# Two stacked graph networks on one core: layer 0 of the next block runs ahead of layer 1, and its rows reach VectorE through SBUF instead of TensorE's transposes

## The chip, the core and the metric

The kernel runs on one core of a Trainium2 chip. The metric is the device time in microseconds (us), the median of several runs. A core has TensorE (PE, the matrix engine), VectorE (DVE), ScalarE (ACT), GpSimd (POOL) and SyncE (SP, which here only issues DMA transfers). Each engine runs its own list of instructions in order, and the lists meet at semaphores only.

## The reference, cut to what matters

The input `x` has 128 graphs of 64 nodes with 384 features, all float32. A first network (two layers) is followed by a residual and a layer norm, then a second network (two layers) with a residual and a layer norm. The change is in the second network:

```python
def layer(h, params):                      # twice
    u = jnp.einsum('bid,bjd->bij', h, h) / temper
    a = jax.nn.softmax(u, axis=-1)
    delta = a * adjacency_matrix
    attn = delta / (jnp.sum(delta, axis=-1, keepdims=True) + 1e-10)
    hl, hs, hr = h @ wl.T + b_l, h @ ws.T + b_s, h @ wr.T + b_r
    ctx = (attn * upper) @ hl + diag(attn)[..., None] * hs + (attn * lower) @ hr
    o = (ctx - mean) / jnp.sqrt(var + LN_EPS) * g + beta
    return jax.nn.relu(o)
```

Both the scores and the values need `h` with the features on the partitions, that is, transposed. For layer 0 the rows come from DRAM (`x1`, the first network's result), for layer 1 from layer 0 of the same block.

## The kernel before

The 8192 rows are cut into 16 blocks of 512 rows (`TOK`), each four tiles of 128. Two blocks ("streams" 0 and 1) make a pass, so there are `PASSES` = 8. Each pass of the second network has four **units** (`UNITS`): layer 0 of stream 0, layer 0 of stream 1, layer 1 of stream 0, layer 1 of stream 1, numbered 0 to 3. The network has 32 units in all. Passes 1 to 6 are a hardware loop on most engines; the others are written out.

TensorE sets the pace. In a unit (`one_pass`, L1244) it folds the score parts (`fold_parts`, L1197), multiplies twelve value products, numbered 0 to 11 (`values`, L1215: nine matmuls each, three sides times four tiles), transposes the exponentials after value 3 if the unit is of layer 1 (`turn_exponentials`, L1208), computes the scores of the next unit (`scores`, L1192), and at last multiplies the four context tiles (`contexts`, L1232).

If the next unit is of layer 1, TensorE also transposes that block's rows between the values: `turn_block` (L1176), twelve transposes of 128x128, eight after value 8 and four after value 9. They read `z`, into which ScalarE's `normalise` (L1363) wrote the rows of layer 0. If the next unit is of layer 0, the rows were loaded from DRAM in quarters (`load_x`, L1123, four transfers) such that VectorE's 32x32 block transposes give the same result: `flip_block` (L1610, three instructions for one unit).

Either way ScalarE then takes the turned block out of PSUM (`turn_out`, L1282) and VectorE writes its low part (`turn_lo`, L1603). In layer 0 ScalarE makes one pass over each of the three parts; in layer 1 it makes two, because gain, shift and relu are applied there (`gain_f`, `shift_f`, a value for each feature).

The four banks `work` form a ring. A value product with a bias needs a bank that ScalarE has filled with the bias (`seed`, L1323), and that waits until VectorE has read the bank four products earlier (`biased_value`, L1627, or `contexts_out`, L1661). So seeds 0 and 1 of a unit wait for VectorE's `contexts_out` of the unit before. ScalarE's order at the start of a unit is `first_half` (L1371). In layer 1 it is seed 0, 1, 3, value 0, the four exponentials, value 1, seed 4. Those exponentials wait for the row maximum, which VectorE takes at the end of the unit before, after `contexts_out` and `variances`, if the next unit is of layer 1 (`begin`, L1847).

After a layer-1 unit its block is finished during the unit that follows: GpSimd applies gain and shift (`times_gain`, `plus_shift`), VectorE adds the residual and takes the last statistics (`add_residual`, L1746, `final_stats`, L1753, `final_var`, L1758), all of it ahead of `contexts_out`; GpSimd normalises one unit later (`final_normalise`, L1546), and SP stores. A unit with this extra work on VectorE is called heavy in what follows. In the kernel before the heavy units are 3 and 0 of the next pass: both are followed by a unit of layer 0.

SP's list (`one_pass`, L1139) loads the residual rows, the next pass's rows and adjacency, and stores the results. The order of work on every engine is written out by hand.

Of the kernel before, what the change touches and what calls it, by code (L numbers as in the profile page):

```python
# [7 lines left out]
ALU = mybir.AluOpType  # L8
# [14 lines left out]
QUADS = P // QUAD  # L23

# [99 lines left out]
def gated_layers(nc, ctx, sh, x, x_t, adj, adj_t, w_left, w_right, w_lin_t, b_lin, ln_a, ln_b, table, x1,  # L124
# [26 lines left out]
    with ExitStack() as overlaid:  # L151
# [98 lines left out]
        def sync_program(sp):  # L250
# [77 lines left out]
            def next_tables():  # L328
                for m in range(3):
                    sp.dma_start(sh.bias[:, m], next_b[m].partition_broadcast(P)).then_inc(next_small, 16)  # L330
                sp.dma_start(sh.gain_f[:], next_ln_w[0].rearrange("(k p) -> p k", p=P),
                             allow_slow_non_contiguous=True).then_inc(next_small, 16)
                sp.dma_start(sh.shift_f[:], next_ln_b[0].rearrange("(k p) -> p k", p=P),
                             allow_slow_non_contiguous=True).then_inc(next_small, 16)
# [661 lines left out]
def softmax_layers(nc, ctx, sh, gated, x1, adj_t, w_nbr_t, table, out):  # L996
# [17 lines left out]
    assert LAYERS == 2 and WN * UNITS % RING == 0 and UNITS * KO % 2 == 0  # L1014
# [8 lines left out]
    with ExitStack() as block_ctx:  # L1023
# [81 lines left out]
        def layer_of(unit):  # L1105
            return unit % UNITS // STREAMS

        def in_layer(i, unit):

            return (i + unit // UNITS) * STREAMS + unit % STREAMS + 1  # L1110
# [6 lines left out]
        def _(sp):  # L1117
            store_last = gated_sync(sp)

            def load_weight(n):  # L1120
                sp.dma_start(stage[n], w_nbr_t[n][1].rearrange("(k p) o -> p k o", p=P)).then_inc(stage_in[n], 16)

            def load_x(i, s):  # L1123
                for q in range(QUADS):
                    sp.dma_start(sh.x_blocks[s][quarter(q)], x_b[i, s, q]).then_inc(x_loaded[s], 16)

            def load_adj(i, s):
                for b in range(2):
                    h = slice(b * 64, b * 64 + 64)
                    sp.dma_start(a_tr[s][h, :, h], adj_t_v[i, s, b]).then_inc(adj_loaded[s], 16)  # L1130
# [3 lines left out]
            load_weight(1)  # L1134
            sp.wait_ge(split, 1)
# [3 lines left out]
            def one_pass(i, last, first=False):  # L1139
                for s in range(STREAMS):  # L1140
                    wait(sp, summed, i * (STREAMS * NT) + (s + 1 - STREAMS) * NT)
                    sp.dma_start(x_res[s][:], x_v[i, s]).then_inc(x_copied[s], 16)
                    if not last:
                        sp.wait_ge(turned, nth(i, s, KO, KO - 1))
                        load_x(i + 1, s)
                for s in range(STREAMS):
                    if not last:
                        sp.wait_ge(keep_ready[s], i + 1)
                        load_adj(i + 1, s)
# [822 lines left out]
```

## Time and profile before

| quantity | value |
|---|---|
| median of 3 runs | 1693.14 us (1692.88 to 1693.48) |
| profiled execution, its own time | 1695.46 us |
| span of that execution, first to last instruction | 1693.6 us |
| mean granted TensorE clock | 0.995 of full speed |
| TensorE busy | 1668.7 us, 99% |
| VectorE busy | 1267.6 us, 75% |
| ScalarE busy | 956.0 us, 56% |
| GpSimd busy | 623.2 us, 37% |

The busy time of an engine counts a stretch in which several of its instructions overlap once. Matmuls overlap, so the mean duration of one is longer than its share of the time. The second network begins at about 839 us of the span and takes the rest. The span and the profiled execution's own time differ by 1.9 us, which lie around the first and the last instruction.

### The profile page before, as it was taken

The page shows a single profiled execution, that of the slowest core. Times are in us where ns is not written, and L with a number is a line of the kernel's source. Part 1 is how long each engine was busy: PE and PEld are TensorE (multiplying, and loading weights), DVE is VectorE, ACT ScalarE, POOL GpSimd, SP SyncE. Part 2 cuts the span into 40 slices and gives each one's busy share as a digit, 9 for nine tenths or more (in the row PEclk, how much of TensorE's full clock was granted, in tenths as well). Part 3 has the DMA queues.
Part 4 walks back from the last instruction along what each step waited for, and adds up shares of the span by engine and source line. Part 5 has one row for each costly group of instructions (what it writes and reads, how often), then busy time and mean ns, then how long its engine had stood idle before and what let it go on. Part 6 is the DMA issues. An engine that isn't in the chain of part 4 may idle for free.

```text
span 1693.6 us, 29852 instructions
## 1 busy us (share of the span) xinstructions
PE 1668.7 (99%) x9684; PEld 1580.2 (93%) x9684; DVE 1267.6 (75%) x2778; ACT 956.0 (56%) x2009; POOL 623.2 (37%) x668
## 2 busy tenths in 40 slices
PE   9999999999999999999999999999999999999995
PEld 8989989889899899899999999999999999999995
DVE  5587685867859678695887968769687686877866
ACT  5645455364554645546566665565655656656654
POOL 5243252433424233243523514434153351523505
PEclk9999999999999999999999999999999999999998
DMA  5215021020300203003104140400304004040101
GB/s 160 77 30 158 6 71 53 25 93 6 109 14 25 93 6 118 6 25 94 49 15 97 41 96 0 118 0 22 96 22 96 0 25 92 22 96 0 49 30 38
DMA packets 108074, 92.02 MB, mean 54 GB/s; under 512 B 63360, under 2 KB 101248, under 8 KB 108032
## 3 DMA queue, kind: packets, MB, share of 16 engines
q1 hardware_dynamic: 108032, 91.51, 19.1%
q8 instruction: 20, 0.33, 0.1%
q14 instruction: 22, 0.18, 0.0%
HBM read 66.33 MB, written 25.17 MB: 54 GB/s over the span
## 4 chain that ended last, share of the span: by engine, by line
PE 93%; DVE 3%; ACT 1%; POOL 1%; DMA 1%; issue 1%; SPq 0%; ACTq 0%; DVEq 0%
PE b_work L1228 33%; PE b_work L377 23%; PE b_work L402 11%; PE b_score_ps L392 8%; PE b_work L1241 8%; PE b_work L413 4%; PE b_score_ps L119 3%; PE b_turn L360 1%; PE b_turn L1185 1%; PE b_score_ps L1204 1%; DMA b_z<-in_L_gnn_W_lin 1%; PE b_score_ps L1201 0%; POOL g_qv_lo L663 0%; PE b_turn L1212 0%; PE b_score_ps L1185 0%
## 5 line engine op out<-in xcount | busy, mean ns | idle before, releaser
L1228 PE MATMUL b_work<-b_w_hi,b_ht 128*128 128x384 f32 x2304 | 605.2, 337 | 0.5 <-ACT b_work L1327 0.3
L1228 PEld LDWEIGHTS b_work<-b_w_hi,b_ht 128*128 128x128 f32 x2304 | 417.5, 188 | 1.7 <-ACT b_work L1327 1.2
L1228 PE MATMUL b_work<-b_w_lo,b_ht 128*128 128x384 f32 x1152 | 385.3, 334 | 0.0
L377 PE MATMUL b_work<-b_ht,b_w_hi 128*128 128x512 f32 x1134 | 350.5, 390 | 0.7 <-DVE g_qv_lo L782 0.7
L663 POOL TENSOR_TENSOR g_qv_lo<-g_v_full,g_qv_hi 128x384 fp32r<-128x384 f32 x128 | 132.8, 1057 | 359.2 <-ACT g_qv_hi L533 359.2
L377 PEld LDWEIGHTS b_work<-b_ht,b_w_hi 128*128 128x128 f32 x1134 | 211.8, 188 | 41.8 <-issue 1.1
L377 PE MATMUL b_work<-b_ht,b_w_lo 128*128 128x512 f32 x567 | 221.6, 391 | 0.0
L1228 PEld LDWEIGHTS b_work<-b_w_lo,b_ht 128*128 128x128 f32 x1152 | 216.5, 188 | 0.0
L1633 DVE TENSOR_TENSOR s_v_lo<-b_work,s_v_hi 128x384 fp32r<-128x384 f32 x256 | 140.7, 555 | 90.3 <-ACT s_v_hi L1333 86.6
L402 PE MATMUL b_work<-b_w_hi,b_ht 128*128 128x384 f32 x768 | 206.1, 335 | 0.0
L1327 ACT ACTIVATE b_work<-b_bias 128x384 f32<-128x384 f32 x256 | 126.4, 494 | 140.0 <-DVE b_z L1671 104.5
L782 DVE TENSOR_TENSOR g_qv_lo<-b_work,g_qv_hi 128x512 fp32r<-128x512 f32 x192 | 128.4, 686 | 98.4 <-ACT g_qv_hi L521 96.5
L521 ACT ACTIVATE g_qv_hi<-b_work 128x512 fp32r<-128x512 f32 x192 | 111.0, 592 | 124.1 <-PE b_work L377 124.0
L1333 ACT ACTIVATE s_v_hi<-b_work 128x384 fp32r<-128x384 f32 x256 | 123.8, 490 | 87.4 <-PE b_work L1228 87.2
L392 PE MATMUL b_score_ps<-g_qv_hi,b_ht 128*128 128x256 f32 x768 | 146.1, 284 | 0.0
L402 PEld LDWEIGHTS b_work<-b_w_hi,b_ht 128*128 128x128 f32 x768 | 139.7, 188 | 1.3
L402 PE MATMUL b_work<-b_w_lo,b_ht 128*128 128x384 f32 x384 | 128.6, 335 | 0.0
L377 PEld LDWEIGHTS b_work<-b_ht,b_w_lo 128*128 128x128 f32 x567 | 106.4, 188 | 22.6
L392 PEld LDWEIGHTS b_score_ps<-g_qv_hi,b_ht 128*128 128x128 f32 x768 | 120.9, 188 | 0.4
L1495 POOL TENSOR_TENSOR s_rstd<-s_var,s_power 128x4 f32<-128x4 f32 x31 | 31.3, 1009 | 235.2 <-DVE s_var L1690 235.2
L525 ACT ACTIVATE g_prob<-g_score_l 128x512 f32<-128x512 f32 x32 | 20.3, 634 | 159.8 <-DVE g_score_l L794 159.8
L392 PE MATMUL b_score_ps<-g_qv_lo,b_ht 128*128 128x256 f32 x384 | 107.2, 279 | 0.0
(174 smaller groups left out, 3288.1 us busy)
## 6 DMA issues: line engine op xcount, KB each, us to landing
g_x_res<-in_x SPq DMA_DIRECT2D x16, 768.0 KB, 7.7
b_x_in<-x SPq DMA_DIRECT2D x64, 192.0 KB, 6.7
s_x_res<-x SPq DMA_DIRECT2D x16, 768.0 KB, 7.3
b_x_in<-in_x_t SPq DMA_DIRECT2D x15, 768.0 KB, 8.9
out<-b_z SPq DMA_DIRECT2D x15, 768.0 KB, 3.8
x<-b_z SPq DMA_DIRECT2D x14, 768.0 KB, 3.9
b_a_tr<-in_adj_t SPq DMA_DIRECT2D x64, 64.0 KB, 3.3
g_a_nat<-in_adj SPq DMA_DIRECT2D x32, 64.0 KB, 2.4
```

The costliest lines, as they stand in the source:

```text
L377: mm = pe.matmul(bank[:], w, h, start=(n == 0), stop=(n == len(pairs) - 1))
L392: mm = pe.matmul(score_ps[:, t, :, :], h, q, start=(n == 0), stop=(n == len(pairs) - 1))
L402: mm = pe.matmul(bank[:, 0:H], h, w, start=(n == 0), stop=(n == len(pairs) - 1))
L413: mm = pe.matmul(bank[:, 0:HC], p[:, t, :], v[:, t, :], start=(n == 0), stop=(n == 2))
L521: nc.scalar.activation(q_hi[:, m, :, d, :], work[use % RING][:], ACT.Copy).then_inc(q_hi_ready, 1)
L663: nc.gpsimd.tensor_tensor(v_lo[:, t, 0:H], v_full[:, t, :], v_hi[:, t, 0:H].bitcast(F32), ALU.subtract).then_inc(v_lo_ready, 1)
L782: op = nc.vector.tensor_tensor(q_lo[:, m, :, d, :], bank, q_hi[:, m, :, d, :].bitcast(F32), ALU.subtract)
L1228: mm = pe.matmul(bank[:, 0:H], h, w, start=(n == 0 and side == 2), stop=(n == len(pairs) - 1), skip_group_check=True)
L1241: mm = pe.matmul(bank[:, 0:HC], p, v, start=(n == 0), stop=(n == len(pairs) - 1))
L1327: nc.scalar.activation(work[(unit * WN + j) % RING][:, 0:H], bias[:, side, layer_of(unit), :], ACT.Copy)\
L1333: nc.scalar.activation(v_hi[:, t, side, 0:H], work[(unit * WN + j) % RING][:, 0:H], ACT.Copy)\
L1633: nc.vector.tensor_tensor(v_lo[:, t, side, 0:H], bank[:, 0:H], v_hi[:, t, side, 0:H].bitcast(F32), ALU.subtract).then_inc(work_free, 1)
```

## The change

The order of the units becomes: layer 0 of block 0, layer 0 of block 1, layer 1 of block 0, layer 0 of block 2, layer 1 of block 1, layer 0 of block 3, ..., layer 0 of block 15, layer 1 of block 14, layer 1 of block 15. So from unit 1 on the layers alternate (odd units layer 0, even units layer 1), up to the last unit, which is of layer 1.

Between layer 0 of a block and its layer 1 there are now two other units instead of one, but for the first and the last block. The normalised rows of layer 0 are copied within SBUF to the layout that `flip_block` wants, by sixteen transfers (`pass_rows_on`), and VectorE turns them. TensorE's `turn_block` stays for the first and the last block alone (`turned_by_tensor`); for these `normalise` writes the rows into `x_in` with the features in the flipped order, and TensorE reads them there. The weights and the gain and shift of layer 1 are loaded in that order too.

```diff
+    def layer_of(i, unit):
+        if serial(i, unit) in (0, FINAL):
+            return int(serial(i, unit) == FINAL)
+        return 1 - unit % 2
+    def turned_by_tensor(i, unit):
+        return serial(i, unit) in (2, FINAL)
...
+            def pass_rows_on(i, unit):
+                k = block_of(i, unit)
+                sp.wait_ge(z_ready, (k + 1) * NT)
+                blocks = sh.x_blocks[1 - unit % 2].rearrange("p (t a) f -> p a t f", a=QUADS)
+                for q in range(QUADS):
+                    for a in range(QUADS):
+                        sp.dma_start(blocks[quarter(q), a], z[unit % 2][quarter(a), :, q * H // QUADS:(q + 1) * H // QUADS])\
+                            .then_inc(x_loaded[1 - unit % 2], 16)
...
+            def one_pass(i):
+                store_out(i - 1, 2)
+                pass_rows_on(i - 1, 3)
+                load_x(i, 3)
+                load_adj(i, 0)
+                load_residual(i, 0)
+                store_out(i, 0)
+                pass_rows_on(i, 1)
+                load_x(i, 5)
+                load_adj(i, 1)
+                load_residual(i, 1)
...
             def second_half(i, unit, more, tail):                # ScalarE
+                turn_next = more and turned_by_tensor(i, unit + 1)
+                early = more and not turn_next and layer_of(i, unit + 1) == 1
+                late = more and layer_of(i, unit + 1) == 0
                 probabilities_hi(i, unit)
+                if early:
+                    turn_out(i, unit + 1, 0)
                 value_hi(i, unit, 6)
                 seed(i, unit, 9)
+                if early:
+                    turn_out(i, unit + 1, 1)
...
             def up_to_contexts(i, unit, last, residual, tail=None):   # VectorE
...
                 probabilities_lo(i, unit)
+                if early:
+                    turn_lo(i, unit + 1, 0)
+                    flip_block(i, unit + 1, 2)
                 biased_value(i, unit, 6)
...
-                layer, s = divmod(unit % UNITS, STREAMS)             # contexts_out
-                if layer == 0 and not first:
-                    dve.wait_ge(stored[s], before[s] + 16 * (i + unit // UNITS))
+                if layer_of(i, unit) == 0:
+                    if serial(i, unit) not in (0, 1):
+                        dve.wait_ge(x_loaded[0], 16 * QUADS * ((k - 1) * QUADS + 1))
+                elif serial(i, unit) not in (2, FINAL):
+                    other = 1 - stream_of(i, unit)
+                    dve.wait_ge(stored[other], before[other] + 16 * (i + unit // UNITS))
```

Smaller parts: GpSimd's `masks` of a stream are made one unit ahead of their use; the loads of layer 1's weights, gain and shift are cut into quarters; SP issues `store_last`, the first network's last stores, at the end of its first pass; TensorE's first pass is written out instead of being part of the loop.

## Rows read from the trace of the kernel before

**Rows 1.** The page, part 1: busy time and share of the span.

```profile
PE 1668.7 (99%) x9684; PEld 1580.2 (93%) x9684; DVE 1267.6 (75%) x2778; ACT 956.0 (56%) x2009; POOL 623.2 (37%) x668
```

**Rows 2.** Busy time, units 2, 3, 0, 1: window, us, PE, PEld, DVE, ACT, POOL, PEclk, DMA.

```profile
1309.78:1336.69 26.91, 26.91 (x169) 26.79 (x168) 17.35 (x39) 16.71 (x38) 6.10 (x5) 1.00 0.00 0
1336.69:1362.25 25.56, 25.56 (x156) 25.53 (x156) 20.76 (x52) 13.46 (x34) 10.31 (x11) 1.00 0.00 0
1362.25:1387.35 25.10, 25.10 (x153) 25.10 (x152) 22.41 (x54) 14.42 (x36) 13.28 (x16) 1.00 0.11 37
1387.35:1413.95 26.60, 26.60 (x164) 26.43 (x164) 19.13 (x42) 17.90 (x41) 9.01 (x10) 1.00 0.67 153
```

**Rows 3.** The chain of waits in unit 2: start us, us, what.

```profile
1324.98 0.87 PE b_turn L1185 x8
...
1327.42 0.44 PE b_score_ps L1185 x4
```

**Rows 4.** Timeline: where a unit begins on TensorE (first fold), start us, us.

```profile
919.37 0.40 PE L1201 MATMUL b_score_ps<-b_part,b_eye_r 128*128 128x256 f32 x2
945.58 0.40 PE L1201 MATMUL b_score_ps<-b_part,b_eye_r 128*128 128x256 f32 x2
1336.53 0.40 PE L1201 MATMUL b_score_ps<-b_part,b_eye_r 128*128 128x256 f32 x2
1387.18 0.40 PE L1201 MATMUL b_score_ps<-b_part,b_eye_r 128*128 128x256 f32 x2
```

**Rows 5.** Timeline of VectorE at the end of unit 0.

```profile
1380.67 0.56 DVE L1633 TENSOR_TENSOR s_v_lo<-b_work,s_v_hi 128x384 fp32r<-128x384 f32 x1 [0.38 <-ACT s_v_hi L1333]
...
1386.72 0.62 DVE L1671 SCALAR_TENSOR_TENSOR b_z<-s_v_own,s_own,b_work 128x385 f32<-128x385 f32 x1
...
1391.97 0.16 DVE L1690 TENSOR_TENSOR s_var<-s_mv,s_total 128x4 f32<-128x4 f32 x1
```

**Rows 6.** Timeline of VectorE and ScalarE in unit 3; unit 2 wasn't heavy.

```profile
1338.66 0.16 DVE L1690 TENSOR_TENSOR s_var<-s_mv,s_total 128x4 f32<-128x4 f32 x1
...
1339.71 0.37 ACT L1314 ACTIVATE s_expo<-b_score_ps,s_exp_bias 128x128 f32<-128x128 f32 x1 [0.23 <-DVE s_exp_bias L1625]
...
1344.70 1.30 ACT L1368 ACTIVATE b_z<-b_z,s_offset,s_rstd 128x384 f32<-128x384 f32 x2
```

**Rows 7.** The chain of waits at the start of unit 3 of pass 0.

```profile
923.59 0.16 DVE s_var L1690
...
924.90 1.51 ACT s_expo L1314 x8
...
926.80 0.39 ACT b_work L1327
...
927.23 12.83 PE b_work L1228 x72
```

**Rows 8.** Waits in that unit: engine, line waited for, us, times, longest.

```profile
PEld b_work L1228 <- ACT b_work L1327: 0.3, 1, 0.3
PEld b_turn L1212 <- ACT s_expo L1314: 0.3, 1, 0.3
```

**Rows 9.** Timeline of ScalarE in the middle of unit 0.

```profile
1371.46 0.48 ACT L1333 ACTIVATE s_v_hi<-b_work 128x384 fp32r<-128x384 f32 x1
...
1373.91 0.49 ACT L1333 ACTIVATE s_v_hi<-b_work 128x384 fp32r<-128x384 f32 x1 [0.59 <-PE b_work L1228]
...
1378.59 0.49 ACT L1333 ACTIVATE s_v_hi<-b_work 128x384 fp32r<-128x384 f32 x1 [1.73 <-PE b_work L1228]
```

**Rows 10.** Operations of turning: duration ns min/median/max, first and last start.

```profile
L1617 DVE STREAM_TRANSPOSE b_score_ps<-b_x_in x45: 699/719/727, 851.8 to 1585.7; 128x512 f32<-128x512 f32 x45
L1292 ACT ACTIVATE b_ht<-b_score_ps,b_shift_f,b_gain_f x16: 795/797/801, 884.5 to 1640.9; 128x512 fp32r<-128x512 f32 x16
```

**Rows 11.** SP's issues of the loads of L1125, and the time to landing.

```profile
L1125 SPq DMA_DIRECT2D b_x_in<-x x56: 348/700/1808, 893.8 to 1509.8; - x56
DMA to landing us min/median/max: 5.3/6.6/7.4
```

More of the change, by code:

```diff
@@ L1137, in _ @@
             sp.wait_ge(split, SIDES)
[L1139 to L1149, printed above, removed]
-                    if first:
-                        store_last(s)
-                    if last and s == STREAMS - 1:
-                        half = NT // 2
-                        for t in range(half):
-                            sp.wait_ge(out_ready, i * (STREAMS * NT) + NT * s + t + 1)
-                            sp.dma_start(out_v[i, s][:, t], z[s][:, t, 0:H]).then_inc(stored[s], 16)
-                            if t == 0:
-                                sp.wait_ge(last_ready, half)
-                                sp.dma_start(out_v[i, s][:, half:], z[s][:, half:, 0:H]).then_inc(stored[s], 16)
-                    else:
-                        sp.wait_ge(out_ready, i * (STREAMS * NT) + NT * (s + 1))
-                        sp.dma_start(out_v[i, s], z[s][:, :, 0:H]).then_inc(stored[s], 16)
@@ L1288, in turn_out @@
                     return
-                bank = turn_banks[k]
+                bank = turn_banks[k] if turned_by_tensor(i, unit) else flipped[k % 2]
                 if layer == 1:
@@ L1577, in one_pass @@
                         weight_lo(2)
-                    if layer == 1 and not last:
-                        final_roots(i, s)
+                    if layer == 1 and not (last and unit == 2):
+                        final_roots(block_of(i, unit), s)
                     if first and unit == 1:
                         gated_final_roots(0)
-                    if not last and unit % STREAMS == 1:
-                        masks(i + 1, unit // STREAMS)
+                    if layer == 0 and unit > 0 and not last:
+                        masks(i + 1, unit // 2)
             pool.wait_ge(sh.next_split, SIDES)
@@ L1821, in up_to_contexts @@
                     gated.final_stats(1, 1)
-                if s is not None and more:
-                    add_residual(i, s, (0, 1))
+                if residual is not None and more:
+                    add_residual(i, residual, (0, 1))
                 biased_value(i, unit, 11)
@@ L1858, in go_on @@
                     gated.final_offset(1)
-                up_to_contexts(i, unit + 1, last, s if layer == 1 else None, unit + 1 if first else None)
+                up_to_contexts(i, unit + 1, last, unit if layer_of(i, unit) == 1 else None, unit + 1 if first else None)
             def lower_layer(i, first=False):
@@ L1916, in _ @@
             gated.gain_and_shift(1)
-            contexts_out(0, 0, first=True)
+            contexts_out(0, 0)
             lower_layer(0, first=True)
```

273 lines of the change are left out of this document (168 added, 105 removed).

## The prediction

> **What bounds the kernel now.** The page comes first: TensorE is busy 99% of the span, VectorE 75%, ScalarE 56% [rows 1]. TensorE is the bound, and the other engines matter only where they make it wait. Next the busy time by stretches, cut where the units of the second network begin [rows 2]. The four units of a pass take 26.91, 25.56, 25.10 and 26.60 us (units 2, 3, 0, 1), 104.17 in all, and TensorE is busy in all of it at a granted clock of 1.00, its upper level of 2.4 GHz. The longer two are those in which it turns the next block. Third, the chain of waits: the twelve transposes stand in it with 0.87 and 0.44 us [rows 3]. Fourth, the timeline and the waits around the start of a layer-1 unit, because there the change puts things together that did not meet before [rows 4 to 8].
>
> **Removed: the transposes on TensorE.** Before, all 16 blocks are turned by TensorE between layer 0 and layer 1; afterwards the first and the last are. That is 14 removed. One costs 1.31 us in the chain (0.87 + 0.44, [rows 3]); two units of layer 1 with and without them differ by 26.91 - 25.56 = 1.35 us [rows 2]. I take 1.35, since it has the changes of bank too: 14 x 1.35 = 18.9 us. Nothing else lies beside these transposes on TensorE, so unhidden they come off the end time. The two units of layer 0 differ by 26.60 - 25.10 = 1.50 [rows 2]: another 0.15 us is a short stall at the start of unit 1, behind a heavy unit. It is in most passes, some 0.8 us in all, and is part of the stall below when the order changes; I count it as given back there.
>
> **Added on VectorE: 42 flips** (14 blocks x 3), 0.72 us each [rows 10], 2.2 us a block. By units: a layer-1 unit now has flips for a unit of layer 0 and no residual; that is less than unit 3 has today (20.76 us of 25.56, [rows 2]), and costs TensorE nothing. A layer-0 unit has the residual of the layer-1 unit before it, and flips. That is the load of unit 0 today: 22.41 us of 25.10, no stall inside it [rows 2]. What is new in it: ScalarE makes two passes over each turned bank instead of one, each 0.8 us [rows 10], so three banks take it about 2.1 us more, placed before value 6, after seed 9 and after seed 10. In unit 0 it has 0.6 us free before value 6, then 0.2, and 1.7 us free before value 9 [rows 9], so values 6 and 7 are read about 0.7 and 1.4 us late. Value 9 is reached about in time: 2.5 us of free time against 2.1. The ring allows the delay: value 10 needs the bank of value 6 some 4.7 us after that is done. At value 10 VectorE is back in step with TensorE (it waits there for ScalarE today, [rows 5]). So inside the unit I price it at 0. If that cover fails by d us, all d goes to TensorE, since the end of the unit has no slack: the stall of 0.15 us shows it.
>
> **Moved: the row maximum behind a heavy unit.** This is the step that costs. In a heavy unit VectorE adds the residual and takes its statistics between value 10 and the first context tile, 6.05 us (1380.67 to 1386.72), and reaches the variance 4.79 us after TensorE began the next unit (1391.97 - 1387.18) [rows 4, 5]. After unit 2, not heavy, it is 2.13 us (1338.66 - 1336.53), and the exponentials begin 1.05 us later [rows 4, 6]. Today a heavy unit is always followed by layer 0, which needs no maximum. Afterwards each layer-1 unit from unit 4 to 30, fourteen in all, stands behind a heavy unit, and ScalarE keeps its order exponentials, value 1, seed 4. TensorE needs the exponentials after value 3 and seed 4 for value 4.
>
> The trace has this meeting once. In pass 0, unit 2 is loaded with the end of the first network. The variance comes at 923.59, 4.22 us into unit 3, the exponentials at 924.90 (5.53), then value 1, seed 4, and the chain goes over from ScalarE to TensorE at 927.23 [rows 4, 7]. TensorE waits 0.3 us for the exponentials and 0.3 us for the seed [rows 8], and the unit takes 945.58 - 919.37 = 26.21 us [rows 4] against 25.56 [rows 2]: 0.65 us. With the variance at 4.79 and 1.05 us to the exponentials they begin at 5.84, 0.31 later: a stall of 0.96 us. Where unit 3 is the heavy one, it ends about 0.3 us earlier than unit 0 (it has no wait for the store before its context tiles), which gives 0.65. I take 0.85: 14 x 0.85 = 11.9 us. Lower end 0 (if VectorE ends earlier), upper end 1.35, where all is eaten.
>
> **Added: sixteen transfers a block,** 15 times. SP issues them when the rows are normalised. Today that is 9.5 us into a layer-1 unit (1344.70 + 1.30 - 1336.53, [rows 4, 6]); with exponentials 2.7 us later, 12. The first flip reads them in the unit after, behind value 3: at 12.83 / 8 = 1.6 us a value [rows 7] that is 7 us in at the earliest. With 25.6 us for the unit between, 20 us are left. The nearest row is the load of the same 768 KB in the same 384-byte pieces, four issues at 0.70 us (0.35 to 1.8) and 6.6 us to landing [rows 11]. Sixteen issues are 6 to 29 us; at 0.7 it is 11.2 + 6.6 = 18 us, hidden. The pieces of one transfer are a quarter in number, so I expect less. In SP's list the next block's rows, the adjacency, the residual rows and the store stand behind; each has a unit or more to spare. `contexts_out` of layer 0 waits for the copy of the last rows to be done, and those of layer 1 for the store of two units before; both are done half a unit before.
>
> **The rest.** The masks are wanted one unit earlier; GpSimd has made them by then, at the end of the layer-1 unit, when it is idle (6.10 us busy in unit 2, [rows 2]). In pass 0, unit 3 no longer needs a maximum and its 0.65 us come back. The weights in quarters, the later `store_last` and the written-out first pass of TensorE lie beside other work: 0, with 1 us either way as my bound.
>
> **The sum,** against the profiled execution: 18.9 + 0.8 + 0.65 - 11.9 = 8.4 us less, so 1695.5 becomes 1687.1 (span 1685.2). The profiled execution stands 2.3 us above the median of the runs, 1693.14; the same difference gives **1685** for the median.
>
> **A rule of the Trainium skill weighed.** The flip in the rows costs 0.72 us for 128x512, three for a block, against 1.31 us of TensorE [rows 3, 10]; in raw engine time VectorE's path is the dearer. "VectorE: DVE Perf Modes", section "Rules for kernel authors", advises TensorE for a 128x128 transpose where the result may lie in PSUM, as here. By that rule the change goes the wrong way, and that is rival C's result; by the rows it is right, since TensorE has no free time and VectorE has.
>
> **The rivals.**
>
> A. *No stall.* VectorE has the variance earlier than in unit 0, because GpSimd's masks no longer run beside it and the unit before was light. Then 20.3 us come off: 1673. For it: the light layer-1 unit before. Against: from value 10 on VectorE's work is fixed and has no gap, 6.05 us. Chance 0.15.
>
> B. *The stall takes about all.* The ring is not recovered by value 7, whose seed was on time by a hair: 1.2 us or more a pair, 1690 to 1696. Chance 0.08.
>
> C. *Slower.* VectorE's and ScalarE's turning in the layer-0 unit is not done by value 10. The delay comes out whole at the end of the unit. My margin is some 0.4 us. The gain is gone at 0.6 us of delay for each block; if the whole 2.2 us of flips is exposed but for the margin, 14 x 1.8 = 25 us are added: 1685 + 25 = 1710. Rival C also takes in the rows that land late, from 0.85 us an issue on (16 x 0.85 + 6.6 = 20): 0.1 us more for each issue is 1.6 us a block, 24 us in all. For it: the largest issue, 1.8 us. Against: the loads before, 0.7. Chance 0.09 for both.
>
> D. *That it doesn't do what it says:* the twelve transposes are surely gone from the list, so I give it nothing of its own.
>
> **How the numbers follow.** Forecast 0.68, A 0.15, B 0.08, C 0.09. The forecast's own range, with the stall from 0.45 to 1.15 us a pair, is 1679 to 1689. The range given is 1672 to 1691: it takes in A and the nearer half of B. 0.2%, or 3.4 us, is about what a measurement of this kernel can tell from no change. Faster by more than that (below 1689.8): forecast, A and a little of B, 0.84. Within: 0.07. Slower: 0.09.
>
> **What would show each step.** In the changed kernel's trace: L1185's successor has 24 transposes instead of 192; units of layer 0 take 25.1 us; layer-1 units 25.6 plus the stall, about 26.4. The waits of TensorE name ScalarE's exponentials and its seed (L1327's successor) 14 times each, with 0.3 to 0.6 us. The exponentials of layer 1 begin 5.5 to 5.8 us after the fold; for rival A it is below 5.0. For rival C, VectorE's flips wait for a DMA, or its first context tile comes later than 0.5 us before the fold. The prediction is wrong if the units of layer 0 are longer than 25.3 us, or if the layer-1 units wait at a place that I have not named.

## The result, and the profile after

The changed kernel takes **1698.49 us** (median of 6 runs, 1695.88 to 1700.32); the kernel before, run beside it, 1692.97 us (6 runs, 1692.39 to 1693.48). The ratio is 1.0033, with a 95% interval of 1.0022 to 1.0044: 0.33% slower. The prediction was 1685 us in a range of 1672 to 1691, and gave slower a chance of 0.09. It was wrong in sign, and the time lies outside its range.

The profiled execution of the changed kernel is its fastest run, 1695.88 us, span 1694.0 us, against 1695.46 and 1693.6 before. Part 1 of its page, then its queues with the fetches of instructions (part 3), its chain (part 4) and the sixteen transfers (part 6) answer to [rows 1] and [rows 11]:

```profile
PE 1658.2 (98%) x9516; PEld 1562.8 (92%) x9516; DVE 1294.8 (76%) x2820; ACT 953.9 (56%) x2009; POOL 621.4 (37%) x668
...
q14 instruction: 42, 0.34, 0.1%
...
PE 79%; DVE 11%; ACT 4%; issue 4%; POOL 1%; DVEq 0%; POOLq 0%; ACTq 0%
...
b_x_in<-b_z SPq DMA_DIRECT2D x224, 48.0 KB, 2.0
```

TensorE has 168 matmuls fewer (9684 - 9516, the 14 x 12 transposes) and is busy 10.5 us less, yet the span isn't shorter: it waits more. The transposes were worth 18.9 us, but a matmul that waits on its way is counted as busy: unit 20 below has 26.48 us of busy TensorE for the work of 25.56. Busy time by units answers to [rows 2]; here are units 17 to 20 (columns: window, us, PE, PEld, DVE, ACT, POOL, granted clock, DMA share, GB/s). Odd units are of layer 0, even ones of layer 1:

```profile
1283.13:1308.23 25.10, 25.10 (x151) 25.10 (x151) 20.10 (x49) 15.69 (x37) 10.17 (x11) 1.00 0.18 43
1308.23:1336.06 27.83, 26.10 (x156) 25.54 (x156) 21.02 (x48) 15.38 (x37) 9.18 (x10) 1.00 0.31 80
1336.06:1361.15 25.09, 25.09 (x151) 25.09 (x151) 19.98 (x49) 15.68 (x37) 10.16 (x11) 1.00 0.16 43
1361.15:1388.29 27.14, 26.48 (x156) 25.51 (x155) 22.21 (x48) 15.34 (x37) 9.21 (x10) 1.00 0.32 81
```

Layer 0 is as forecast. Layer 1 was forecast at 26.4 us and takes 27.0 to 27.2 in ten units, 27.8 in four (10, 14, 18 and 22), counting unit 30 without its own transposes. A layer-1 unit without a stall takes 25.56 us [rows 2], so the fourteen are 24.3 us over it in all, where the prediction had 11.9. The traces close with it: from the first unit's start to the last one's it was 809.7 us before; less 20.35 (18.9 + 0.8 + 0.65, the prediction's own sum of what goes) plus 24.3 is 813.7, as measured. TensorE's waits, answering to [rows 8] (engine, line waited for, us in total, times, longest):

```profile
PEld b_work L1305 <- ACT b_work L1405: 18.1, 22, 2.0
PE b_work L1305 <- ACT b_work L1405: 13.0, 17, 1.7
PEld b_turn L1289 <- ACT s_expo L1392: 4.5, 14, 0.4
```

The exponentials (L1392) are there as forecast, 14 times with 0.3 us each. The seeds (L1405) were forecast with 14 waits of 0.3 to 0.6; they have 22 on the weight loads alone, and up to 2.0 us.

**A second stall in ten layer-1 units.** Unit 20 begins at 1361.15. Its timeline, VectorE first, then GpSimd, ScalarE, TensorE (start us, us, engine, line, operation; in brackets the idle time ahead and what ended it), answers to [rows 6]:

```profile
1365.85 0.16 DVE L1786 TENSOR_TENSOR s_var<-s_mv,s_total 128x4 f32<-128x4 f32 x1
...
1369.75 1.22 DVE L1808 SCALAR_TENSOR_TENSOR s_offset<-s_mv,s_rstd 128x4 f32<-128x4 f32 x1
1370.89 1.28 DVE L1741 TENSOR_TENSOR b_turn<-b_turn,s_keep 128x512 f32<-128x512 f32 x2
...
1369.65 1.30 POOL L1581 TENSOR_TENSOR s_expo<-s_expo,s_keep 128x512 f32<-128x512 f32 x1
...
1366.89 0.37 ACT L1392 ACTIVATE s_expo<-b_score_ps,s_exp_bias 128x128 f32<-128x128 f32 x1 [1.18 <-DVE s_exp_bias L1717]
...
1371.01 1.31 ACT L1451 ACTIVATE b_z<-b_z,s_offset,s_rstd 128x384 f32<-128x384 f32 x2 [0.64 <-DVE s_offset L1808]
...
1374.16 0.48 ACT L1405 ACTIVATE b_work<-b_bias 128x384 f32<-128x384 f32 x1
...
1374.69 0.44 PE L1305 MATMUL b_work<-b_w_hi,b_ht 128*128 128x384 f32 x1 [0.52 <-ACT b_work L1405]
```

The variance comes 4.70 us into the unit and the exponentials 5.74, both as the prediction had them. But the layer norm's offset (L1808), an operation on 128x4 values, takes 1.22 us instead of 0.15. It starts 0.10 us behind GpSimd's product for the diagonal (L1581, 1.30 us) and ends with it (1370.97 against 1370.95). ScalarE's `normalise` (L1451) waits for the offset, the seed of value 7 stands behind it at 1374.16, and TensorE waits. The offset's line in the two traces (duration ns min/median/max):

```profile
L1808 DVE SCALAR_TENSOR_TENSOR s_offset<-s_mv,s_rstd x31: 150/153/1352, 869.9 to 1657.3; 128x4 f32<-128x4 f32 x31
```

```profile
L1712 DVE SCALAR_TENSOR_TENSOR s_offset<-s_mv,s_rstd x31: 152/154/998, 871.6 to 1655.0; 128x4 f32<-128x4 f32 x31
```

The second is the kernel before. Its longest offset, 998 ns, ends with a GpSimd operation too (L1470, in unit 1). The median hides more: in fourteen other units, 4, 5, 8, 9 and so on to 29, all of layer 0, the offset took 0.37 to 0.47 us, and each time it ended with one of GpSimd's four `final_normalise` operations (L1549, 0.67 us each). In unit 20 of before:

```profile
1367.87 1.96 POOL L1549 TENSOR_SCALAR b_z<-b_z,s_frstd,s_foffset 128x384 f32<-128x384 f32 x3
1368.14 0.40 DVE L1712 SCALAR_TENSOR_TENSOR s_offset<-s_mv,s_rstd 128x4 f32<-128x4 f32 x1
```

After the change ten of 31 are over 1.2 us, all in layer-1 units. In the four units at the loop's edge (next finding) the offset comes only when the product is done, and takes 0.15.

The Trainium skill has a rule for this ("SBUF — State Buffer", section "SBUF: two separate sides"): VectorE and GpSimd share a pair of ports that is locked for a whole instruction, and a VectorE operation with two SBUF inputs that meets a running GpSimd operation that reads SBUF waits until that one is done. The rows agree: the offset reads two tiles of SBUF and ends with GpSimd's product, while in the experiment below VectorE's L1742 (the same line as L1741 here), which takes one of its inputs from PSUM, runs beside the same product at its usual length.

**A halt of VectorE in four units.** The chain around the start of unit 18 (start us, us, what):

```profile
1313.75 0.06 DVEq L2021
1313.81 2.73 issue
1316.54 0.06 DVEq L2021
...
1316.65 0.57 DVE s_v_lo L1725
...
1317.24 0.50 ACT b_work L1405
```

L2021 is VectorE's hardware loop over the passes of the second network: five turns, passes 1 to 5, and so four back edges, in units 10, 14, 18 and 22. At this back edge VectorE issues nothing for 2.73 us and is idle for 2.82; before, it was idle for 0.36. The packets of instructions (q14) went from 22 to 42, 8 KB each: five for every turn, in which the loop is fetched anew. In the window 1080 to 1500 us, which lies inside the loop, the queue has no packet before the change, and after it

```profile
q14 instruction: 20, 0.16, 0.1%
```

One of them is the only DMA traffic of the core during the 2.73 us of this halt. The kernels below bear it out: the eleven with 42 or 43 packets halt for 2.7 to 3.7 us at every back edge, the four with a loop and 22 or 23 packets for 0.3 to 0.4. So the fetch and the halt go together everywhere, which is as near as these runs come to showing that one makes the other.

### The profile page after: what moved, and what is told of

Read it like the earlier page. It is cut to its first block, busy times and chain, and to the rows that moved or that the text cites. A ratio compares the mean times of both kernels' runs of the same rounds, so it can differ in the third digit from the quotient of the medians.

```text
span 1694.0 us, 29820 instructions
## 1 busy us (share of the span) xinstructions
PE 1658.2 (98%) x9516; PEld 1562.8 (92%) x9516; DVE 1294.8 (76%) x2820; ACT 953.9 (56%) x2009; POOL 621.4 (37%) x668
## 3 DMA queue, kind: packets, MB, share of 16 engines
q1 hardware_dynamic: 140528, 102.54, 21.4%
## 4 chain that ended last, share of the span: by engine, by line
PE 79%; DVE 11%; ACT 4%; issue 4%; POOL 1%; DVEq 0%; POOLq 0%; ACTq 0%
PE b_work L1305 25%; PE b_work L378 23%; PE b_work L403 11%; PE b_score_ps L393 8%; PE b_work L414 4%; PE b_work L1318 4%; DVE b_z L1767 2%; PE b_score_ps L120 1%; DVE s_fstats L1853 1%; DVE b_z L1847 1%; PE b_turn L361 1%; ACT s_v_hi L1411 1%; ACT b_z L1451 1%; DVE s_v_own L1729 1%; DVE s_stats L1770 1%
## 5 line engine op out<-in xcount | busy, mean ns | idle before, releaser
L1405 ACT ACTIVATE b_work<-b_bias 128x384 f32<-128x384 f32 x256 | 127.6, 499 | 150.9 <-DVE b_z L1767 104.9
L1570 POOL TENSOR_TENSOR s_keep<-b_a_tr,b_const 128x512 f32<-128x512 f32 x48 | 60.8, 1297 | 164.2 <-DVE s_own L1751 164.2
```

What stands on the lines that cost most here:

```text
L1405: nc.scalar.activation(work[(unit * WN + j) % RING][:, 0:H], bias[:, side, layer_of(i, unit), :], ACT.Copy)\
```

## The experiments

Two theories at the start: (1) the offset beside GpSimd's product makes the second stall; (2) the halt at the loop's edge comes from where or how long the loop is in VectorE's program. Their rivals: (3) the ring isn't recovered whatever the offset does (the prediction's rival B); (4) the fetches come from the change's own waits. The expectations number their theories anew. Medians stand beside the kernel before, timed on the same chip.

**The offset ahead of GpSimd's product** (behind value 0 in layer-1 units):

```diff
                 for j in range(SIDES):
                     biased_value(i, unit + 1, j)
-                deviations(i, unit)
+                    if j == 0 and layer_of(i, unit + 1) == 1:
+                        deviations(i, unit)
+                if layer_of(i, unit + 1) == 0:
+                    deviations(i, unit)
```

> The changed kernel, but in a layer-1 unit VectorE computes the 128x4 offset behind value 0 instead of behind value 2, so before GpSimd multiplies the exponentials by the diagonal mask. Theory (the offset takes 1.22 to 1.35 us instead of 0.15 because it starts 0.1 us after that 128x512 product of GpSimd, and ScalarE's normalise, value 4 and seed 7 are late by it): the offset is back at 0.15 us, TensorE's stall before value 7 (0.78 to 0.91 us in nine or ten of the fourteen units) falls below 0.2, the one before value 4 (0.6) stays. Units 4, 6, 8 ... take 26.3 instead of 27.1 us, some 8 us less in all: 1690 to 1691. Rival (seed 7 is late only because the exponentials are late): the second stall stays at 0.8 and the time at 1698.

Measured: 1695.35 us, ratio 1.0003 (0.9993 to 1.0013). Units 16 and 18:

```profile
1256.03:1282.46 26.43, 26.29 (x155) 25.52 (x155) 21.48 (x48) 15.26 (x37) 9.19 (x10) 1.00 0.32 84
1307.56:1337.19 29.63, 27.69 (x156) 27.13 (x155) 21.64 (x48) 15.43 (x37) 9.14 (x10) 0.94 0.34 84
```

The second stall is gone in the ten units (26.2 to 26.5 us). The offset isn't quite back at 0.15 us, as I had expected: at its new place it takes 0.17 to 0.50 beside `final_normalise`, but it is early enough there. Most of what that gives is lost again at the loop's edge: 28.3 to 29.6 us, in three of four with a granted clock of 0.94 over the unit. In unit 18 TensorE's first matmul after the halt and the third pair, here and then in the changed kernel:

```profile
1317.32 0.44 PE L1305 MATMUL b_work<-b_w_hi,b_ht 128*128 128x384 f32 x1 [1.91 <-ACT b_work L1405]
...
1318.82 0.84 PE L1305 MATMUL b_work<-b_w_hi,b_ht 128*128 128x384 f32 x2
```

```profile
1317.79 0.44 PE L1305 MATMUL b_work<-b_w_hi,b_ht 128*128 128x384 f32 x1 [1.71 <-ACT b_work L1405]
...
1318.77 0.51 PE L1305 MATMUL b_work<-b_w_hi,b_ht 128*128 128x384 f32 x2
```

And the granted clock in the same stretch, here and in the changed kernel:

```profile
1317.50:1327.00 9.50, 9.50 (x46) 9.50 (x47) 7.35 (x14) 7.83 (x16) 0.00 (x0) 0.82 0.35 103
```

```profile
1318.00:1327.00 9.00, 9.00 (x53) 9.00 (x53) 7.59 (x15) 7.78 (x16) 0.00 (x0) 1.00 0.39 117
```

TensorE waited 1.91 us and then ran part of the time at the lower of its levels (1.2 GHz; a mean of 0.82 of 2.4 GHz is a mix of both); a pair of matmuls took 0.84 us instead of 0.51. In the changed kernel it waited 1.71 us and the clock held. Over the unit it is 27.69 us of busy TensorE for the work of 26.29. The length of the wait doesn't decide it, though. Here are units 10 and 18 of the kernel in which GpSimd's product waits (a2, below):

```profile
1096.33:1124.47 28.14, 26.09 (x156) 25.53 (x155) 21.02 (x48) 15.37 (x37) 9.22 (x10) 1.00 0.31 80
1305.78:1335.19 29.41, 27.69 (x156) 27.13 (x155) 21.32 (x48) 15.42 (x37) 9.20 (x10) 0.94 0.38 87
```

TensorE waited 2.01 us in the first and 1.71 in the second.

**VectorE's loop turned by one unit**, so that its edge lies ahead of a layer-0 unit:

```diff
-            lower_layer(1)
+            begin(1, 0)
             with dve.Fori(1, PASSES - 2) as i:
+                go_on(i, 0)
+                begin(i, 1)
                 upper_layer(i)
-                lower_layer(i + 1)
-            upper_layer(PASSES - 2)
+                begin(i + 1, 0)
+            go_on(PASSES - 2, 0)
+            begin(PASSES - 2, 1)
+            upper_layer(PASSES - 2)
```

> The changed kernel with VectorE's hardware loop turned by a unit, so that its back edge lies ahead of a layer-0 unit, where VectorE has slack, and not between the row maximum and value 0 of a layer-1 unit. Nothing else moves. Theory (at the edge VectorE has no instructions for 2.7 us, because the longer loop body is fetched again each time): the 2.7 us are still in the trace at the edge, four times, but behind them TensorE doesn't wait; the four units of 27.83 us become 27.1, 2.8 us less in all. Rival (the 2.7 us are a wait for something of that place, ScalarE's values or GpSimd): they stay where they are, or vanish altogether, with 0 or over 3 us of change.

Measured: 1698.26 us, ratio 1.0026 (1.0016 to 1.0036). The halt moved with the edge, but wasn't hidden: the layer-0 unit behind it takes 25.9 instead of 25.1, the next one 27.4.

**The last statistics later:** those of the finished block move from the heavy unit into the layer-1 unit behind it, GpSimd's roots and `final_normalise` with them.

```diff
-                    final_stats(i, residual)
-                    final_var(block_of(i, residual))
...
                 for j in range(SIDES):
                     biased_value(i, unit + 1, j)
+                    if finish is not None and j == 0:
+                        final_stats(i, finish, (0, 1))
                 deviations(i, unit)
+                if finish is not None:
+                    final_stats(i, finish, (2, 3))
+                    final_var(block_of(i, finish))
```

> The changed kernel, but the last statistics of a block (four bn_stats, four aggregations, the variance; 2.4 us of VectorE) go from the layer-0 unit, ahead of its context tiles, to the layer-1 unit behind it: two behind value 0, two behind the offset; GpSimd takes the last root and the last normalisation after them. Theory (the whole stall comes from VectorE ending the layer-0 unit 2.4 us later than a light unit): first context tile 3.0 us before the fold instead of 0.5, exponentials 3.2 us after it instead of 5.6, both stalls at 0, layer-1 units 25.6 us: 22 us less in the second network, 1673 to 1677 by the median. The edge of VectorE's loop still costs 2.7 us of VectorE, hidden or nearly (up to 3 us in all). Rival (TensorE's transposes removed give nothing because the ring or the copies bound the unit): layer-1 units stay above 26.5 us.

Measured: **1673.02 us**, ratio 0.9873 (0.9856 to 0.9889), faster than both kernels. Layer-1 units take 25.55, layer-0 units 25.10, no stall is left, and the exponentials begin at 3.2 us. It shows 22 fetches and no halt, though its loop is longer (343 instructions a turn against 339 in the changed kernel).

**Is it the loop's length?** The kernel before, with twenty spare 128x4 memsets on VectorE in the loop.

> The kernel before, with twenty memsets of a spare 128x4 tile (62 ns each) added to VectorE's loop in the middle of unit 2, where VectorE waits anyway. It makes the loop body as long as that of the changed kernel. Theory (a body over some length is fetched again at each turn): the step over the back edge, 0.36 us in the kernel before, becomes about 2.7 us, and there are about 20 more instruction fetches of 8 KB on the queues; the total hardly moves, since unit 2 of the kernel before has slack there. Rival (the 2.7 us come from something else in the changed kernel): the edge stays at 0.36 us and the fetches at their number.

Measured: one run, 1694.27 us, 22 fetches, 0.36 us at the edge, with 339 instructions a turn, as many as the changed kernel has. Length alone is not the cause; my theory fell.

**GpSimd's product waits for the offset**, VectorE's order unchanged:

```diff
                     pool.wait_ge(exp_turned, in_layer(i, unit))
+                    pool.wait_ge(offset_ready, nth(i, unit - 1, 1, 0))
```

> GpSimd's diagonal product for a layer-1 unit waits until VectorE's offset for that unit has been written; VectorE's order is that of the changed kernel. Theory (the offset is slow only because GpSimd's product runs beside it): the offset takes 0.15 us again in all layer-1 units instead of 1.22 to 1.35, although it stands at the same place; normalise and the seeds behind it come 1.1 us earlier, the stall before value 7 (0.8 us) goes, the one before value 4 stays; ten layer-1 units at about 26.3 us instead of 27.1; the four at the loop edge of VectorE unchanged at 27.8. Time about 1690. Rival (the offset is slow because it waits for something of its own, or the stall before value 7 is that of ring and seeds whatever the offset does): the offset stays over 1 us or the units stay at 27.1; time 1698. A third way: the product, 1.3 us later, delays the own terms of the scores on TensorE; then a wait on GpSimd appears in its place.

Measured: 1694.89 us, ratio 0.9999 (0.9989 to 1.0009). The offset is back at 153 ns at the same place, and the ten units take 26.2 to 26.4. That is theory 1, and rival 3 falls. The units at the edge take 28.1 to 29.6, not 27.8 as expected, and that eats most of it: 1694.9 where 1690 was expected.

**The maximum first**, right behind `contexts_out` in `up_to_contexts`, ahead of `final_offset` and the variances instead of behind them.

> The row maximum of a layer-1 unit stands right behind the context tiles, ahead of the last statistics' offset and of the variances. Theory: maximum and so exponentials come earlier by what stands between, 0.6 us of small operations, so exponentials at 5.0 us instead of 5.6 after the unit's first matmul; the stall before value 4 falls from 0.6 to about 0; but the offset stays beside GpSimd's product, so the stall before value 7 stays or grows (TensorE is there earlier): units 26.5 to 27.0, time 1690 to 1696. Rival (the prediction's: one stall, set by the maximum alone): the whole stall goes and layer-1 units take 25.6 to 25.9, time 1680.

Measured: 1690.85 us, ratio 0.9979 (0.9969 to 0.9988). The exponentials begin at 4.8 to 4.9, a little earlier than expected, and the ten units take 25.55 to 25.73: both stalls go. My expectation that the offset would stay slow was wrong: in the ten units it takes 0.20 to 0.41 us. In unit 16 it now starts 7.8 us into the unit (8.6 before the edit) and the product at 9.2 (8.5 before), so they don't meet. The product is later because GpSimd's list there is the root of the variance, `final_normalise` and then the product, and the variance, now behind the maximum, comes 0.74 us later. So this run doesn't price the maximum's place alone: it takes the second stall away too. The four edge units take 28.5 to 30.0 (window of unit 18, with its neighbour 16):

```profile
1253.91:1279.63 25.72, 25.72 (x156) 25.58 (x155) 21.12 (x48) 15.27 (x37) 9.24 (x10) 1.00 0.34 87
1304.73:1334.62 29.89, 27.44 (x155) 27.16 (x155) 21.50 (x48) 15.42 (x37) 9.17 (x10) 0.94 0.36 85
```

**Which place makes the fetches?** Spare memsets on VectorE in the changed kernel: 20 in each turn of the loop; 20 ahead of the second network; 52 there; and 20 + 20 in the kernel before.

```diff
             gated.variances()
+            for n in range(PAD):
+                nc.vector.memset(spare[:, n * NT:(n + 1) * NT], 0.0)
             probabilities(0, 0)
```

> The changed kernel with twenty spare 128x4 memsets in each turn of VectorE's loop (about 17 ns each). The kernel before showed 0.36 us at the loop's back edge with 306 and with 326 instructions in the loop; the changed kernel 2.73 us and five instruction fetches of 8 KB a turn with 321. Theory 1 (the place of the loop's end in the stream of instructions decides whether its head is still held): with 341 the fetches fall or change in number, and the edge may be 0.4 us: units at the edge 27.1 instead of 27.8, time 1695. Theory 2 (something in the changed kernel's loop, its waits or the time at which VectorE reaches the edge, causes the fetches): twenty fetches again, 2.7 us an edge, time 1698 to 1699.

> The changed kernel with the twenty spare memsets ahead of the second network instead, once. The loop is unchanged but starts twenty instructions further on. Theory 1 (place of the loop in the stream): the fetches at the edge go or change in number. Theory 2: 42 fetch packets and 2.7 us an edge as before.

> The changed kernel with 52 spare memsets on VectorE ahead of the second network's loop, once (some 1 us, 840 us before the end, in cover). Counted with its register instructions, VectorE's program has 1376 instructions in the kernel before and is fetched in 22 packets, so one packet of 8 KB holds about 64. Theory 1 (packets of 64 are kept, and the loop is held only if with what is fetched ahead of its end it touches no more than six): the kernels with a loop of 339 to 343 that show no fetches in the loop begin it at instruction 746 or 747 of the program, those that show them at 758 and 778 (and 694, a packet less than 758). 52 more is 810, which stands in its packet as 746 does: the twenty fetches and the 2.7 us at four edges are gone, units at the edge 27.1 instead of 27.8 us, the granted clock does not dip there; time 1695 to 1696, 3 us below the changed kernel's 1698.5. Theory 2 (cause in the loop's own waits or timing): 42 packets and 27.8 us as before.

> The kernel before with twenty spare memsets in each turn of VectorE's loop and twenty ahead of the loop: 339 instructions that begin at 766, between the 758 and 778 at which the changed kernel fetches. Theory 1: this kernel, without anything of the change, now shows twenty fetches more in the loop (42 packets instead of 22) and 2.7 us at the back edge; TensorE may be covered from it in part, time 1694 to 1700. Theory 2 (the change's waits or timing): 22 packets, 0.36 us at the edge.

Measured: 1700.41 us (ratio 1.0039, 1.0025 to 1.0053), 1700.96 (one run) and 1700.93 (1.0047, 1.0031 to 1.0064), each with 42 fetches; the arithmetic by packets of 64 was wrong. The fourth is the telling one: the kernel before, with nothing of the change, now has 42 fetches. VectorE's first value behind the edge, with the twenty in the loop alone:

```profile
1311.96 0.56 DVE L1635 TENSOR_TENSOR s_v_lo<-b_work,s_v_hi 128x384 fp32r<-128x384 f32 x1 [0.36 <-issue]
```

and with twenty ahead of it as well:

```profile
1314.28 1.02 DVE L1635 TENSOR_TENSOR s_v_lo<-b_work,s_v_hi 128x384 fp32r<-128x384 f32 x2 [2.81 <-ACT s_v_hi L1335]
```

These two kernels differ only in twenty memsets that run once, ahead of the second network. So rival 4 falls: with the loop's length the same, its place in VectorE's program switches the fetches on. Five packets come in each of its turns up to the last back edge, so one run tells it. The unit on TensorE stays at 26.90 there and the time at 1692.75 us (one run), because in that order VectorE comes to the edge early (variance at 2.14 us). The change moves the edge behind a heavy unit (4.59 us), where nothing covers it.

**Both effects taken away, first try,** with the 52 memsets ahead:

> Both of the effects that the prediction lacked are taken away and nothing else: the 52 spare memsets ahead, and GpSimd's diagonal product waits for the offset. If the account of the error is complete, what is left is the prediction's own stall: layer-1 units of 26.2 to 26.4 us, all of them, those at the loop edge too, and 1684 to 1688 us. If theory 1 on the fetches is wrong: 1695 as the kernel with the waiting product alone. If something else is missing in the account: edge units normal and yet over 1689.

> The 52 spare memsets ahead, and the row maximum right behind the context tiles. With the maximum first alone the ten layer-1 units away from the edges took 25.55 to 25.73 us and the four at the edges 28.5 to 30.0 (3.1 us of issue at the edge, and the clock at 0.94 in the unit). Theory 1: without the fetches all fourteen take 25.6 to 25.9, the mean clock is over 0.995, and the time is 1675 to 1678. Theory 2: 1691 as without the memsets.

Measured: 1694.4 us (ratio 1.0006, 0.9996 to 1.0016) and 1687.31 (0.9967, 0.9955 to 0.998). As the fetches stayed, these test only the edge again: in the first, unit 18 takes 29.40 us at a clock of 0.94.

**No back edge.** VectorE's loop is written out (f1), with GpSimd's waiting product (f2), with the maximum first (f3); and 104 spare memsets ahead of the loop kept as a loop (f4).

```diff
-            with dve.Fori(1, PASSES - 2) as i:
+            for i in range(1, PASSES - 2):
                 upper_layer(i)
                 lower_layer(i + 1)
```

> VectorE's loop over passes 1 to 5 of the second network is written out, all else as in the changed kernel. Theory (the halt belongs to the jump back, since the head of the loop is no longer held): no stretch of 2.7 us in which VectorE issues nothing, units 10, 14, 18 and 22 take 27.0 to 27.15 as their neighbours instead of 27.8; 4 x 0.7 = 2.8 us less in the profiled execution, and the clock no lower; 1695 us, ratio 1.001. Rival (instructions are fetched late wherever they are new; the long stretch costs more fetches, about 35 to 40 packets in all, with halts of their own): halts at other places, 1698 or more.

> The loop written out, and GpSimd's diagonal product waits for the offset: both effects that the prediction lacked are gone. If the account is complete, all layer-1 units take 26.2 to 26.4 us, and the time is the prediction's 1684 to 1688. If something else is missing, it is over 1689 with normal edges.

> The loop written out, and the maximum right behind the context tiles: fourteen layer-1 units of 25.55 to 25.75 us, clock over 0.995; 1675 to 1678, near the kernel with the late statistics (1673). With the loop it was 1691: then four halts have cost 13 to 15 us, though each is only 2.7 to 3.1 us long, because TensorE reaches the edge sooner and the clock falls there.

> The changed kernel with 104 spare memsets on VectorE ahead of the second network. If what holds the loop is its place in the stream with a period of 128 (a memset being one instruction there, others on average two), 104 stands where the unfetched kernels stand: 22 packets, no halt. If not: 42 packets again, and the rule of the place stays open.

Measured:

| kernel | us, median | ratio (95%) | layer-1 units | fetches |
|---|---|---|---|---|
| f1 no loop | 1692.53 | 0.9996 (0.9986 to 1.0005) | 26.95 to 27.31 | 28 |
| f2 and waiting product | 1681.76 | 0.9929 (0.9913 to 0.9946) | 26.21 to 26.58 | 29 |
| f3 and maximum first | 1673.81 | 0.9884 (0.9868 to 0.9901) | 25.55 to 25.90 | 28 |
| f4 104 ahead, loop kept | 1694.66 (one run) | | 26.98 to 27.13 | 23 |

Unit 18 in f1, and then in f2:

```profile
1306.89:1333.86 26.97, 26.31 (x155) 25.45 (x155) 21.92 (x48) 15.33 (x37) 9.19 (x10) 1.00 0.32 82
```

```profile
1301.63:1327.87 26.24, 26.13 (x156) 25.51 (x155) 20.81 (x48) 15.26 (x37) 9.25 (x10) 1.00 0.32 83
```

And the start of a layer-1 unit in f2, VectorE, then GpSimd: the offset ahead of the product, 0.15 us, and L1742 beside the product at 0.65 each:

```profile
1310.04 0.15 DVE L1809 SCALAR_TENSOR_TENSOR s_offset<-s_mv,s_rstd 128x4 f32<-128x4 f32 x1
1310.11 1.29 DVE L1742 TENSOR_TENSOR b_turn<-b_turn,s_keep 128x512 f32<-128x512 f32 x2
...
1310.34 1.30 POOL L1582 TENSOR_TENSOR s_expo<-s_expo,s_keep 128x512 f32<-128x512 f32 x1 [0.32 <-DVE s_offset L1809]
```

f4 keeps the loop and loses the halt: unit 18 takes 27.04 us. Its span is 2.05 us longer ahead of the second network's unit 1, which the memsets there cost; less these it is 1692.6, the time of f1. Its expectation, a period of 128 memsets, came true in one run; a rule isn't shown by that.

## Why the prediction was wrong

By its steps:

- **Removed, right.** Fourteen blocks' transposes and two small stalls were to give 18.9 + 0.8 + 0.65 = 20.35 us. With all stalls gone, f3 is 19.4 us under its kernel before (1693.21 - 1673.81), and the late statistics 21.4 (1694.39 - 1673.02).
- **Flips and double passes in the layer-0 units, right:** 25.10 us, no stall. Rival C fell: VectorE turned 14 blocks more at 0.72 us a flip and TensorE never waited for it in layer 0. The change did turn out slower, as by the rule of the Trainium skill that the prediction weighed ("VectorE: DVE Perf Modes", section "Rules for kernel authors"), but not for what the rule compares: without the stalls VectorE's path is the faster one here, by the 19.4 to 21.4 us above.
- **Sixteen transfers, right:** hidden, 2.0 us to landing; VectorE waits for none. They run for 14 blocks (224 issues), not 15.
- **"Moved: the row maximum behind a heavy unit", the step that failed.** What it counted was close: exponentials at 5.5 to 5.7 us (5.5 to 5.8 forecast), and the stall alone, measured in f2, is 26.24 - 25.56 = 0.68 us a unit, 9.5 us in 14, where 11.9 was said. What it didn't count is the rest of VectorE's and ScalarE's delayed list. The offset, late by 2.3 to 2.5 us (at 8.4 to 8.6 us of the unit, 6.1 before), meets GpSimd's product, and the seed of value 7 comes late by it. f1 against f2 prices that: 1692.53 - 1681.76 = 10.8 us, 0.77 a unit. Rival B said that value 7 would be late and gave it 1690 to 1696 and 0.08; it had the place, but not the cause: with the offset in front of the product the ring is recovered. The row that the prediction leaned on, unit 3 of pass 0 [rows 7], couldn't show it: there the product starts 13.6 us into the unit and the offset at 8.4. In the changed kernel's layer-1 units the product starts at 8.3 to 8.5.
- **"The rest", priced at 0 with 1 us as a bound, also failed:** VectorE's loop got another length and place, and its back edge now stands in a unit without cover. The prediction doesn't name that loop. 2.7 us of halt cost 0.8 us in each of four units in the profiled execution (27.82 against 27.03 in f4). By medians the loop costs 1698.49 - 1692.53 = 6.0 us, though these were timed in different sessions. About 4 of it is seen in the units: from unit 0 to unit 31 it is 813.66 us in the changed kernel and 809.62 in f1; 3.1 of that is in the four edge units, and 0.9 in units 8, 12, 16, 20 and 24, which are 0.16 to 0.20 shorter without the loop. The other 2 us aren't shown in a trace of the changed kernel. They probably go with the clock: four of its six runs have a mean clock of 0.993 or 0.994 and 1697.9 to 1700.3 us, while its profiled, fastest run has 0.995 and f1's ten runs 0.995 or 0.996; against it, one run of 1698.1 us has 0.995 too. The kernel with twenty memsets ahead shows how such a run can look: its units 10 and 22 have a clock of 0.94 and take 29.4 and 29.6 us instead of 27.8.

The prediction's own mechanism, with nothing beside it, is f2: 1681.76 us, 11.45 under its kernel before, where 8.4 was forecast. The sum gives 1693.2 - 20.35 + 9.5 = 1682.4 for it. With the two missed effects it is 1693.0 - 20.35 + 9.5 + 10.8 + 6.0 = 1698.9 for the changed kernel, against 1698.5; its last two terms are differences between that kernel, f1 and f2, so only the part up to f2 tests anything. Of the 13.5 us between forecast and result, the two missed effects are 10.8 + 6.0, and the first stall, taken too large, gives 2.4 back: 14.4, which is 0.9 too much and within what medians of different sessions can tell (the kernel before alone is 1692.97 to 1694.39 by session). Left open: by what rule the loop's place leads to fetches, and what makes the clock fall at some edges and not at others.

How the trace of before could have told it: its offset line shows 998 ns once in 31, and fourteen more took 0.37 to 0.47 us, each ending with a GpSimd operation. The prediction read ScalarE's list down to seed 4 and stopped there; of the operations that a late variance delays, the offset was next.

## What to carry to other kernels

When a step is delayed, follow every operation behind it on its engine through the whole unit, and ask what now runs beside it on GpSimd. A maximum in a line of durations that is six times its median is worth looking up: here it was a meeting of two engines, which the change made the rule. Look at the instruction fetches after each change of a hardware loop, and keep its back edge where the engine is ahead. To make room, move work out of the heavy unit rather than arrange the waits behind it: the late statistics turned a loss of 0.3% into a gain of 1.3%. The early maximum gained 0.2% with the loop kept and 1.2% with it written out.

## What the runs showed of the hardware that I had not expected

- A 128x4 operation of VectorE on two SBUF tiles took 1.22 to 1.26 us instead of 0.15, beside a 1.30 us product of GpSimd that started 0.05 to 0.11 us ahead; with the product behind it, 0.15. It took 1.35 in unit 4, where it started beside one GpSimd operation and 0.04 us ahead of the product, and ended with the product. In the trace of before and in three after it (the changed kernel, the early offset, the early maximum) every one of these offsets over 0.19 us ends within 0.03 us of the end of a GpSimd operation.
- A hardware loop of VectorE can be held or fetched anew every turn: 22 packets or 42, 0.36 us at the edge or 2.7 to 3.7. Twenty spare instructions ahead of it switched the fetching on (the kernel before, with twenty more in the loop), 104 ahead of it switched it off (the changed kernel); 20 and 52 did not.
- A wait of TensorE at the loop's edge was followed in some units by a granted clock of 0.94 over the unit, and TensorE busy some 1.5 us more (27.69 against 26.09, and 27.44 against 25.91, in units of one kernel), and in others not; its length doesn't tell them apart. The clock fell after 1.68, 1.71, 1.75 and 1.91 us and held after 1.71, 2.01 and 2.64. It fell at 14 of 20 edges in the five traces in which one of the other stalls had been removed, and at 2 of 16 in the four in which both were there (the changed kernel and those with 20, 20 and 52 spare memsets; the turned loop, whose edge is elsewhere, isn't counted). The kernel with the maximum first has a mean clock of 0.991 to 0.993, with the loop written out 0.995 to 0.996.
